# Attention stage of a four-layer graph network: output rows of source nodes made inside the steps, weights taken with the new running maximum

## The chip, the cores and the metric

The kernel runs on one core of a Trainium2 chip. The metric is the device time of one launch in microseconds. Three runs of the kernel before took 2148.57, 2148.97 and 2158.34 us; their median is 2148.97 us.

## The reference, cut to what matters

Four graph layers run one after the other on 10,000 nodes of 512 features and 2,500 edges; each is added to its input and normalised by row. The change is in the last, an attention of 8 heads in which every edge's weight is normalised over the edges that have the same source node:

```python
q, k, v = jnp.split(x @ W, [512, 1024], axis=-1)
aw = jnp.einsum('ehf,ehf->eh', (q * scaling)[src], k[dst])
m = segment_max(aw, src);  e = jnp.exp(aw - m[src])
alpha = e / segment_sum(e, src)[src]
out = segment_sum(alpha[:, :, None] * v[dst], src)
x = layernorm(x + out)          # all 10,000 rows are the output
```

A node that is no edge's source has out = 0, so its row needs none of this.

## The kernel before, in words

**Phases.** Phases follow one another with a barrier between: messages of layer 0, its dense part, `aggregate_phase` and `edge_rows_phase` for layers 1 and 2, and then `values_phase` (names f_), which does the attention. The change is in that last phase, from 1643 us on, but for one loop in `aggregate_phase` that marks which edges are the first of their source (L1103 to L1109, into `k.unique`).

**Two works in one loop.** `values_phase` has `STEPS` = 24 steps. In them run (a) 20 edge tiles of 128 edges, each passing through five stages in five steps (letters a to e in the code, so that tile d of step s is tile s - 3), and (b) 40 pairs of row blocks (2 x 128 rows), the output rows without attention. The edge tiles gather rows of both ends (L1666), finish layer 2 for them (L1976, L1873 to L1881), multiply by W on PE (queries L1770, values L1798, keys L1776), take the scores of 8 heads (L1989), the largest of each source in the tile (L2000, L2006), the weights exp(score - maximum) on ACT (L1906), weighted values (L2017) and their sums per source on PE (L1806).

**A running state in DRAM.** For each source node the table `state` holds 520 sums and 8 maxima. For tile t, POOL gathers the old rows (`gather_state`, L1672), DVE takes the new maximum (L2025), ACT two sets of factors (L1912), DVE scales the old sums and the tile's sums and adds them (L2038 to L2048), and POOL scatters the rows back (`scatter_state`, L1677). The gather of tile t + 1 waits for the scatter of tile t to land. The weights do not wait for the gather.

**Pairs.** `plain_plan` says how many pairs DVE handles in each step: 3, 3, 2, 2, then 2 and 1 in turn, at the end 1 and 2. Four buffers hold them (`ROW_BUFS`). For a pair, SP fills the buffer with a constant row (`pair_fill`, L1224), POOL adds the rows of table p by an accumulating DMA (`pair_add_p`, L1231), DVE scales, rectifies and adds x1 (L1253 to L1272), ACT normalises its two tiles (`tile_normalise`, L1282 to L1287, five operations each), and SP stores it (L1242). A fill waits until the store of the pair four before has landed. The first `PLAIN` = 3 pairs are loaded directly.

**Order.** Every engine works through its own list in order; a wait holds back all that stands behind it. On POOL a step is: scatter of the state, gather of the next state, gathers of rows for two steps on, and the adds for the pairs of the next step, each waiting for its fill. ACT normalises, in a step, tiles of earlier pairs (`tile_plan`): a third early, a third in the middle, and the last one behind the rows of L1881.

**The last loop.** After the steps, ten groups of two tiles follow: POOL gathers the final sums per edge (L1707), DVE divides, adds the residual row and takes its mean and variance (L2083 to L2104), ACT normalises (L1955), and POOL scatters the rows to the output (L1716), where only the first edge of a source writes.

Of the kernel before, what the change touches and what calls it, by code (L numbers as in the profile page):

```python
# [30 lines left out]
P = 128  # L31
# [24 lines left out]
PLAIN = 3  # L56
# [857 lines left out]
def aggregate_phase(nc, k):  # L914
# [4 lines left out]
    with phase(nc, "a_") as (sb, ps, sem), ExitStack() as ctx:  # L919
# [138 lines left out]
        def _(dve):  # L1058
# [44 lines left out]
            ready(nc.vector.memset(seen[:, 0:1], 0.0))  # L1103
# [113 lines left out]
def pair_fill(nc, k, sp, j):  # L1217

    b = j % ROW_BUFS
    if j >= ROW_BUFS:  # L1220
        sp.wait_ge(k.pair_gone[b], 16 * (j // ROW_BUFS))
    else:
        sp.wait_ge(k.quotient_done, 1)
    sp.dma_start(k.pair_rows[b][:, :, :], k.quotient[:, :].rearrange("p (a d) -> p a d", a=1).to_broadcast([P, 2, D])  # L1224
                 ).then_inc(k.pair_filled[b], 16)
# [65 lines left out]
def edge_rows_phase(nc, k):  # L1291

    tail_buffers(nc, k)
    with phase(nc, "e_") as (sb, ps, sem), ExitStack() as ctx:
# [36 lines left out]
        def _(sp):  # L1331
# [11 lines left out]
            pair_fill(nc, k, sp, PLAIN)  # L1343
# [235 lines left out]
def values_phase(nc, k):  # L1579
# [4 lines left out]
    with phase(nc, "f_") as (sb, ps, sem), ExitStack() as ctx:  # L1584
# [19 lines left out]
        fall, factor = sb("fall", [P, 2, HEADS]), sb("factor", [P, 2, HEADS])  # L1604
# [14 lines left out]
        weighed, v_done, vw_done, s_done, old_in, new_top, fall_done, factors, scaled, part_done, merged, gone = (  # L1619
            sem(n) for n in ("weighed", "v_done", "vw", "s_done", "old_in", "new_top", "fall", "factors", "scaled",  # L1620
                             "part", "merged", "gone"))


        G, SUM_BUFS = T // 2, 3
        sums = [k.filters[:, :, :, :].rearrange("p t c f -> p (t c f)")[:, i * 2 * STATE:(i + 1) * 2 * STATE].rearrange(
            "p (s w) -> p s w", s=2) for i in range(SUM_BUFS)]
        inv = [sb(f"inv{i}", [P, 2, HEADS]) for i in range(2)]
        o_stats, o_mv = ([sb(f"o_{n}{i}", [P, 2, w]) for i in range(2)] for n, w in (("stats", 6), ("mv", 2)))
        o_neg, o_rstd, o_shift = ([sb(f"o_{n}{i}", [P, 2]) for i in range(2)] for n in ("neg", "rstd", "shift"))
        sums_in = [sem(f"sums_in{i}") for i in range(SUM_BUFS)]  # L1630
        out_gone = [sem(f"out_gone{i}") for i in range(ROWS_AHEAD)]
        inv_done, att, o_y_done, st, mv_done, o_ready, o_sc, out_done = (
            sem(n) for n in ("inv", "att", "o_y", "st", "mv", "o_ready", "o_sc", "out"))
# [12 lines left out]
        def _(sp):  # L1646
# [10 lines left out]
            for b in range(ROWS_AHEAD):  # L1657
                sp.wait_ge(out_gone[b], 32 * len(range(b, G, ROWS_AHEAD)))

        @block.gpsimd  # L1660
        def _(pool):
# [17 lines left out]

            gather_rows(0)  # L1680
# [8 lines left out]
            for step in range(STEPS):  # L1689
# [7 lines left out]
                if step + 1 < STEPS:  # L1697
                    for j in range(given, given + HERE[step + 1]):
                        pair_add_p(nc, k, pool, j)
                    given += HERE[step + 1]  # L1700
            pool.wait_ge(gone, 16 * T)

            def gather_sums(g):
                if g >= SUM_BUFS:
                    pool.wait_ge(att, 2 * (g - SUM_BUFS + 1))
                for s in range(2):
                    pool.indirect_dma_start(sums[g % SUM_BUFS][:, s, :], None, k.state[:, :],  # L1707
                                            at_rows(k.index[:, 0, 2 * g + s:2 * g + s + 1])
                                            ).then_inc(sums_in[g % SUM_BUFS], 16)

            def scatter_rows(g):
                for s in range(2):
                    t = 2 * g + s
                    pool.wait_ge(out_done, t + 1)

                    pool.indirect_dma_start(k.out[:, :], at_rows(k.unique[:, 1, t:t + 1]), y[g % ROWS_AHEAD][:, s, :],  # L1716
                                            None, bounds_check=N - 1, oob_is_err=False
                                            ).then_inc(out_gone[g % ROWS_AHEAD], 16)

            for g in range(SUM_BUFS):  # L1720
                gather_sums(g)

            for b in range(ROW_BUFS):
                pool.wait_ge(k.pair_gone[b], 16 * (PAIRS // ROW_BUFS))
            for g in range(G):
                if g + SUM_BUFS < G:
                    gather_sums(g + SUM_BUFS)
                scatter_rows(g)

        @block.tensor  # L1730
        def _(pe):
# [50 lines left out]
            def spread_scores(t):  # L1782

                pe.wait_ge(aw_out, t + 1)
                if t:
                    pe.wait_ge(part_done, t)
# [47 lines left out]
        def _(act):  # L1834
# [73 lines left out]
            def state_factors(t):  # L1908
                act.wait_ge(fall_done, t + 1)
                if t:  # L1910
                    act.wait_ge(part_done, t)
                nc.scalar.activation(factor[:, :, :], fall[:, :, :], ACT.Exp).then_inc(factors, 1)  # L1912
# [3 lines left out]
            for step in range(STEPS + 1):  # L1916
# [8 lines left out]
                if 0 <= e < T:  # L1925
                    state_factors(e)
# [23 lines left out]
            for g in range(G):  # L1950
                b, rows = g % 2, y[g % ROWS_AHEAD]
                act.wait_ge(o_ready, g + 1)
                reciprocal_deviation(nc, k, act, o_mv[b][:, :, 1], o_neg[b], o_rstd[b][:, :], o_shift[b], o_sc, 4 * g)
                for s in range(2):
                    nc.scalar.activation(rows[:, s, :], rows[:, s, :], ACT.Identity, bias=o_shift[b][:, s:s + 1],  # L1955
                                         scale=o_rstd[b][:, s:s + 1]).then_inc(out_done, 1)

        @block.vector
        def _(dve):
# [34 lines left out]
            def tile_maximum(t):  # L1994
# [11 lines left out]
                nc.vector.tensor_reduce(top, cand[:, :, :], AX_X, ALU.max).then_inc(top_done, 1)  # L2006
                dve.wait_ge(top_done, t + 1)
                if t:
                    dve.wait_ge(weighed, t)
                nc.vector.tensor_tensor(less[:, :], k.scores[:, t, :], top, ALU.subtract).then_inc(less_done, 1)  # L2010

# [9 lines left out]
            def new_maximum(t):  # L2021
                buf, top = old[t % 2], new[:, ATT:STATE]
                dve.wait_ge(old_in, 16 * (t + 1))
                dve.wait_ge(top_done, t + 1)
                nc.vector.tensor_tensor(top, buf[:, ATT:STATE], buf[:, STATE:STATE + HEADS], ALU.max  # L2025
                                        ).then_inc(new_top, 1)
                dve.wait_ge(new_top, t + 1)
                if t:
                    dve.wait_ge(factors, t)
                nc.vector.tensor_tensor(fall[:, :, :], buf[:, ATT:STATE + HEADS].rearrange("p (a h) -> p a h", a=2),  # L2030
                                        top.rearrange("p (a h) -> p a h", a=1).to_broadcast([P, 2, HEADS]),
                                        ALU.subtract).then_inc(fall_done, 1)

            def merge(t):
                wide = lambda i: factor[:, i, :].rearrange("p (h a) -> p h a", a=1).to_broadcast([P, HEADS, HD + 1])
                dve.wait_ge(factors, t + 1)
                dve.wait_ge(s_done, t + 1)
                nc.vector.tensor_tensor(state_parts(new), state_parts(old[t % 2]), wide(0), ALU.mult  # L2038
                                        ).then_inc(scaled, 1)
                if t:  # L2040
                    dve.wait_ge(merged, t)
                nc.vector.tensor_tensor(
                    part[:, :, :].rearrange("p (a h) f -> p a h f", a=2),
                    p_S[:, :, 0:ATT // 2].rearrange("p a (h f) -> p a h f", h=HEADS // 2),
                    wide(1).rearrange("p (a h) f -> p a h f", a=2), ALU.mult).then_inc(part_done, 1)
                dve.wait_ge(scaled, t + 1)
                dve.wait_ge(part_done, t + 1)
                nc.vector.tensor_tensor(state_parts(new), state_parts(new), part[:, :, :], ALU.add).then_inc(merged, 1)  # L2048

            pair = 0  # L2050
            for step in range(STEPS):
# [3 lines left out]
                if 0 <= e < T:  # L2055
                    new_maximum(e)
# [17 lines left out]

            dve.wait_ge(x3_done, 2 * T)
            for g in range(G):
                b, c, rows = g % 2, g % SUM_BUFS, y[g % ROWS_AHEAD]
# [160 lines left out]
```

## Time and profile before

| what | us |
|---|---|
| median of three runs | 2148.97 |
| the profiled execution | 2156.94 |
| its span, first to last instruction | 2155.2 |
| first pair in `values_phase` | 1643.3 |
| weights of the first edge tile | 1719.0 |
| weights of the last edge tile | 2070.2 |
| start of the last loop's first gather | 2083.8 |

In the profile a row of the timeline is an instruction or several alike in a run; what stands in brackets is how long its engine had been idle and what ended that. In the chain of waits each row was released by the one above it. A DMA's row there lasts from its issue to its landing. PE, ACT, DVE and POOL are compute engines; SP only issues DMAs.

### The profile page before, as it was taken

How to read it: one execution, taken by the hardware profiler on the slowest of the kernel's cores; microseconds unless marked ns; L12 is line 12 of the kernel's file. 1: busy time of each engine (PE TensorE's matmuls, PEld its weight loads, DVE VectorE, ACT ScalarE, POOL GpSimd, SP SyncE). 2: the span in 40 equal slices, each digit the busy share in tenths (PEclk: the TensorE clock that was granted, in tenths of full speed). 3: DMA queues.
4: the chain of work that ended last, by engine and by line, in shares of the span. 5: the costliest groups of instructions: out<-in, count | busy, mean ns of one | idle time of the engine just before them, and what ended most of it. 6: DMA issues, size and time to landing. Idle time of an engine off the chain costs nothing. (4 is left out here: it accounts for less than half of the span.)

```text
span 2155.2 us, 24520 instructions
## 1 busy us (share of the span) xinstructions
PE 1803.9 (84%) x5525; PEld 933.2 (43%) x5525; DVE 1434.7 (67%) x2621; ACT 1149.2 (53%) x2356; POOL 949.1 (44%) x1070
## 2 busy tenths in 40 slices
PE   5999999599999999999999995961881588998840
PEld 2444444244444444444444443531771344544420
DVE  5365554177777777777777773517995578787876
ACT  1344434255555555555555552224883878877853
POOL 2212102166666666656666663544553232333236
PEclk8999999799999999999999997985555689999965
DMA  7752102534444454444444445554556887878774
GB/s 250 250 206 63 27 13 31 142 134 172 171 159 166 157 172 172 165 164 155 169 172 172 163 153 188 105 87 156 110 119 178 257 242 221 238 212 241 200 212 144
DMA packets 167421, 350.61 MB, mean 163 GB/s; under 512 B 30481, under 2 KB 30962, under 8 KB 166838
## 3 DMA queue, kind: packets, MB, share of 16 engines
q1 hardware_dynamic: 130838, 247.28, 32.4%
q0 software_dynamic: 33168, 98.01, 20.4%
q10 hardware_dynamic: 3344, 4.51, 0.7%
q8 instruction: 28, 0.46, 0.1%
q14 instruction: 43, 0.35, 0.1%
HBM read 177.32 MB, written 153.71 MB: 154 GB/s over the span
## 5 line engine op out<-in xcount | busy, mean ns | idle before, releaser
L687 PE MATMUL d_p_h<-w3a,d_xT 128*128 128x512 f32 x632 | 285.6, 595 | 23.2 <-DMA d_xT<-in_xT 23.2
L687 PE MATMUL d_p_p<-d_wr,d_x1T 128*128 128x512 f32 x632 | 288.3, 600 | 0.0
L687 PE MATMUL d_p_o<-d_w,d_uT 128*128 128x512 f32 x632 | 284.5, 593 | 3.0 <-ACT d_uT L762 3.0
L562 POOL TENSOR_SCALAR d_small<-d_mv 128x1 f32<-128x1 f32 x158 | 77.6, 491 | 296.7 <-DVE d_mv L813 148.7
L851 DVE TENSOR_TENSOR d_zz<-d_yg,d_xbeta 128x512 f32<-128x512 f32 x79 | 136.9, 1733 | 96.3 <-POOL d_yg L902 96.3
L687 PEld LDWEIGHTS d_p_h<-w3a,d_xT 128*128 128x128 f32 x632 | 120.7, 191 | 175.6 <-issue 175.6
L687 PEld LDWEIGHTS d_p_o<-d_w,d_uT 128*128 128x128 f32 x632 | 119.8, 190 | 153.7 <-issue 149.1
L755 ACT ACTIVATE d_yn<-d_y,d_small 128x512 f32<-128x512 f32 x79 | 64.3, 814 | 228.2 <-POOL d_small L567 228.2
L687 PEld LDWEIGHTS d_p_p<-d_wr,d_x1T 128*128 128x128 f32 x632 | 115.6, 193 | 116.5 <-issue 116.5
L783 ACT ACTIVATE d_x<-d_zz,d_small 128x512 f32<-128x512 f32 x79 | 64.2, 813 | 174.9 <-POOL d_small L567 174.9
L294 PE MATMUL m_p_H<-m_xT,m_w 128*128 128x512 f32 x320 | 146.8, 613 | 4.8 <-ACT m_xT L335 4.8
L511 DVE TENSOR_SCALAR m_h<-m_p_H,m_bias 128x512 f32<-128x512 f32 x40 | 30.0, 750 | 153.2 <-issue 96.9
L388 ACT ACTIVATE m_den<-m_low 128x512 f32<-128x512 f32 x40 | 25.2, 630 | 188.3 <-DVE m_low L516 188.3
L564 POOL TENSOR_TENSOR d_small<-d_small,minus_half 128x1 f32<-128x1 f32 x158 | 116.1, 735 | 13.2
L1762 PE MATMUL f_p_qv<-filters,same_dst 128*128 128x512 f32 x160 | 88.3, 704 | 32.6 <-ACT same_dst L1842 32.4
L902 POOL TENSOR_TENSOR d_yg<-d_yn,d_gamma_row 128x512 f32<-128x512 f32 x79 | 114.5, 1450 | 0.0
L896 POOL TENSOR_TENSOR d_xb<-d_x,d_b_row 128x512 f32<-128x512 f32 x79 | 100.0, 1266 | 12.5 <-DMA d_x<-in_x 12.5
L221 POOL DMA_INDIRECT sum_counted<-m_tile_sum,unique x20 | 31.4, 1568 | 167.4 <-ACT m_tile_sum L351 150.3
L208 POOL DMA_INDIRECT m_x_in<-in_x,index x40 | 44.3, 1108 | 137.5 <-PE m_p_T L250 123.0
L844 DVE TENSOR_SCALAR d_low<-d_h 128x512 f32<-128x512 f32 x79 | 101.5, 1285 | 2.7
L883 POOL TENSOR_TENSOR d_xbeta<-d_x,d_beta_row 128x512 f32<-128x512 f32 x79 | 100.3, 1270 | 0.0
L806 DVE TENSOR_TENSOR d_y<-d_p_o,d_xb 128x512 f32<-128x512 f32 x79 | 54.6, 691 | 66.9 <-PE d_p_o L687 66.9
(286 smaller groups left out, 4080.9 us busy)
## 6 DMA issues: line engine op xcount, KB each, us to landing
sum_counted<-m_tile_sum SPq DMA_DIRECT2D x10, 2112.0 KB
state<-d_empty SPq DMA_DIRECT2D x80, 264.0 KB, 2.4
update<-d_empty SPq DMA_DIRECT2D x80, 256.0 KB, 2.3
pair_x<-x SPq DMA_DIRECT2D x40, 512.0 KB
out_rows<-pair_rows SPq DMA_DIRECT2D x40, 512.0 KB
d_xT<-in_xT SPq DMA_DIRECT2D x79, 256.0 KB
d_z<-sum_counted SPq DMA_DIRECT2D x79, 256.0 KB
d_x<-in_x SPq DMA_DIRECT2D x79, 256.0 KB
```

What stands on the lines that cost most here:

```text
L294: pe.matmul(out, w1[:, s * KB + b, cols], xT[:, g % 2, s, b, :], start=(s == 0 and b == 0), stop=False)
L562: nc.gpsimd.tensor_scalar(tmp, var, factor, add, ALU.mult, ALU.add).then_inc(done, 1)
L564: nc.gpsimd.tensor_tensor(rstd, tmp, k.minus_half[:, 0:1], ALU.pow).then_inc(done, 1)
L687: last = nc.tensor.matmul(out[:, :], lhsT[:, c, :], w[:, c, :], start=(c == 0), stop=(c == KB - 1))
L755: nc.scalar.activation(yn[b][:, :], y[b][:, :], ACT.Identity, bias=small[b][:, 0, 2:3], scale=small[b][:, 0, 1:2]).then_inc(yn_done, 1)
L783: nc.scalar.activation(x1[b][:, :], zz[b][:, :], ACT.Identity, bias=small[b][:, 1, 2:3], scale=small[b][:, 1, 1:2]).then_inc(x1_done, 1)
L844: nc.vector.tensor_scalar(low[b][:, :], h[b][:, :], MISH_ONE, None, ALU.min).then_inc(low_done, 1)
L851: nc.vector.tensor_tensor(zz[b][:, :], yg[b][:, :], xbeta[b][:, :], ALU.add).then_inc(zz_done, 1)
L883: nc.gpsimd.tensor_tensor(xbeta[b][:, :], x[b][:, :], beta_row[:, :], ALU.add).then_inc(xbeta_done, 1)
L896: nc.gpsimd.tensor_tensor(xb[b][:, :], x[b][:, :], b4_row[:, :], ALU.add).then_inc(xb_done, 1)
L902: nc.gpsimd.tensor_tensor(yg[b][:, :], yn[b][:, :], gamma_row[:, :], ALU.mult).then_inc(yg_done, 1)
L1762: last = nc.tensor.matmul(out[:, :], xT[:, c, :], w[:, c, :], start=(c == 0), stop=(c == KB - 1))
```

## The change

Source rows are finished in the step in which their tile is merged (`attend` on DVE, `source_rows` on ACT), in place in `k.src_rows_sb`; the last loop is gone. `k.unique` now marks the last edge of each source, whose merged sums are final. All output scatters stand in the last three steps of POOL's list (8, 9 and 3 of them), behind a wait for all pair stores, so the pairs are moved to 2 in each of the first 20 steps and none after. The weights of a tile are taken against the new running maximum, so `new_maximum` moves into the step of `tile_maximum`, behind the first pair's means, and the merge is one product and one sum. `PLAIN` is 4.

```diff
 def plain_plan(steps):
-    plan = [3, 3, 2, 2] + [2 - i % 2 for i in range(steps - 6)] + [1, 2]
+    plan = [2] * (steps - 4) + [0] * 4
 def tile_plan(plan):
-        n = given - done if step < 5 or step == len(plan) else min(given - done, 3)
+        n = given - done if step < 5 or step == len(plan) else min(given - done, 4)
 # aggregate_phase, DVE
-            for t in range(1, T):
-                ready(nc.vector.tensor_scalar(equal[:, 0:t * P], rows_i[:, 0:t * P], col_f[:, 0, t:t + 1], None,
+            for t in range(T - 1):
+                later = min((t + 1) * P, LAST_START)
+                ready(nc.vector.tensor_scalar(equal[:, later:E], rows_i[:, later:E], col_f[:, 0, t:t + 1], None,
                                               ALU.is_equal, ALU.add, accum_out=seen[:, t:t + 1]))
 # values_phase, POOL: steps as before, then
+                if step == STEPS - 3:
+                    for b in range(ROW_BUFS):
+                        pool.wait_ge(k.pair_gone[b], 16 * (PAIRS // ROW_BUFS))
+                if step >= STEPS - 3:
+                    for i in range(WRITTEN[step - STEPS + 3], WRITTEN[step - STEPS + 4]):
+                        scatter_out(i)
 # ACT
                 if 0 <= d < T:
                     weights(d)
+                    state_factors(d)
                 if 0 <= b < T:
                     x3_squares(b, 0)
                     x3_squares(b, 1)
                     x3_rows(b)
+                if 0 <= e < T:
+                    source_rows(e)
 # DVE
             def new_maximum(t):
                 dve.wait_ge(old_in, 16 * (t + 1))
...
+                nc.vector.tensor_tensor(less[:, :], k.scores[:, t, :], top, ALU.subtract).then_inc(less_done, 1)
             def merge(t):
+                nc.vector.tensor_tensor(state_parts(new), state_parts(old[t % 2]), wide, ALU.mult).then_inc(scaled, 1)
+                nc.vector.tensor_tensor(halves, halves, p_S[:, :, 0:ATT // 2], ALU.add).then_inc(merged, 1)
+            def attend(t):
+                nc.vector.reciprocal(inv[:, :], state_parts(new)[:, :, HD]).then_inc(inv_done, 1)
...
+                nc.vector.bn_stats(o_stats[b][:, :], row).then_inc(st, 1)
...
                 if 0 <= e < T:
-                    new_maximum(e)
                     merge(e)
...
                 if 0 <= d < T:
+                    new_maximum(d)
                     weigh_values(d)
                 if a < T:
                     softplus(a)
+                if 0 <= e < T:
+                    attend(e)
```

On POOL, one step in the middle before. `f_y` are gathered rows, `pair_rows<-p_rows` the add of a pair, `state<-f_new` the scatter of the state, `f_old<-state` its gather; this step has one add.

```order
L1666 DMA f_y<-update,index 128x512 x2
L1231 DMA pair_rows<-p_rows 128x1024
L1677 DMA state<-f_new,unique 10240x528
L1672 DMA f_old<-state,index 128x528
L1666 DMA f_y<-update,index 128x512 x2
L1231 DMA pair_rows<-p_rows 128x1024 x2
```

The same place in the changed kernel.

```order
L1658 DMA f_y<-update,index 128x512 x2
L1230 DMA pair_rows<-p_rows 128x1024 x2
L1669 DMA state<-f_new,unique 10240x528
L1664 DMA f_old<-state,index 128x528
L1658 DMA f_y<-update,index 128x512 x2
L1230 DMA pair_rows<-p_rows 128x1024 x2
```

Two adds now stand ahead of every scatter of the state up to step 19, where one and two took turns.

On DVE, the middle of a step before, from the tile's candidates to the weighted values (`f_old<-filters` is the tile's maximum, `f_less` what ACT makes weights of).

```order
L2000 TENSOR_TENSOR filters<-f_p_S,f_away 128x1024
L2006 TENSOR_REDUCE f_old<-filters 128x8
L2010 TENSOR_TENSOR f_less<-scores,f_old 128x8
L1269 SCALAR_TENSOR_TENSOR pair_rows,pair_total<-pair_x,pair_rows 128x512 x2
L1272 TENSOR_SCALAR pair_neg<-pair_total 128x2
L2017 TENSOR_TENSOR f_both<-f_p_qv,f_both 128x8x64
```

The same place in the changed kernel, with `attend` behind it.

```order
L1978 TENSOR_TENSOR filters<-f_p_S,f_away 128x1024
L1984 TENSOR_REDUCE f_old<-filters 128x8
L1268 SCALAR_TENSOR_TENSOR pair_rows,pair_total<-pair_x,pair_rows 128x512 x2
L1271 TENSOR_SCALAR pair_neg<-pair_total 128x2
L1991 TENSOR_TENSOR f_new<-f_old 128x8
L1996 TENSOR_TENSOR f_less<-scores,f_new 128x8
L1999 TENSOR_TENSOR f_fall<-f_old,f_new 128x8
L2006 TENSOR_TENSOR f_both<-f_p_qv,f_both 128x8x64
L1942 TENSOR_SCALAR f_pos<-f_y 128x256
L1946 SCALAR_TENSOR_TENSOR f_ssp<-f_logs,f_pos 128x256
L2026 RECIPROCAL f_inv<-f_new 128x8
L2030 TENSOR_TENSOR f_part<-f_new,f_inv 128x8x64
```

`f_less` now reads `f_new`, which reads the gathered `f_old`, and stands behind the pair's means; `attend` begins with the last two rows.

## Rows read from the trace of the kernel before

**Rows 1.** One line's instructions, weights of the 20 edge tiles on ACT (duration, first and last start).

```profile
L1906 ACT ACTIVATE f_both<-f_less x20: 215/216/219, 1719.0 to 2070.2; 128x8 f32<-128x8 f32 x20
```

**Rows 2.** Chain of waits, 1890 to 2040 us (start, time, engine or DMA, what).

```profile
1896.53 6.77 PE f_p_qv L1762 x8
...
2016.13 1.23 DVE filters L2000
...
2026.47 3.71 PE f_p_qv L1762 x8
...
2033.09 1.24 DVE filters L2000
```

**Rows 3.** Chain of waits, 1728 to 1743 us.

```profile
1728.63 5.38 DMA pair_rows<-pair_quotient
1734.30 0.91 POOL pair_rows L1231
1735.51 6.20 DMA state<-f_new,unique
1741.97 1.05 POOL f_old L1672
```

**Rows 4.** Timeline of DVE near 1730 us (start, time, line, what, [idle before]).

```profile
1729.59 0.70 DVE L2048 TENSOR_TENSOR f_new<-f_new,f_part 128x520 f32<-128x520 f32 x1
```

**Rows 5.** Timeline of DVE, first pair of two steps.

```profile
1693.88 1.23 DVE L1253 TENSOR_TENSOR pair_rows<-pair_rows,bn_scale 128x1024 f32<-128x1024 f32 x1 [4.82 <-DMA pair_rows<-p_rows]
...
1711.24 1.23 DVE L1253 TENSOR_TENSOR pair_rows<-pair_rows,bn_scale 128x1024 f32<-128x1024 f32 x1 [4.06 <-DMA pair_rows<-p_rows]
```

**Rows 6.** Timeline of ACT, weights and the step's last row tile.

```profile
2018.85 0.21 ACT L1906 ACTIVATE f_both<-f_less 128x8 f32<-128x8 f32 x1 [0.94 <-DVE f_less L2010]
...
2023.20 0.71 ACT L1282 ACTIVATE pair_scratch<-pair_rows,pair_neg 128x512 f32<-128x512 f32 x1
...
2024.92 0.81 ACT L1287 ACTIVATE pair_rows<-pair_rows,pair_shift,pair_rstd 128x512 f32<-128x512 f32 x1
```

**Rows 7.** Timeline of SP's DMA issues, stores and the fills behind them.

```profile
1794.76 0.34 SPq L1242 DMA_DIRECT2D out_rows<-pair_rows  x1
1797.89 0.60 SPq L1224 DMA_DIRECT2D pair_rows<-pair_quotient  x1
...
1954.57 0.34 SPq L1242 DMA_DIRECT2D out_rows<-pair_rows  x1
1961.64 0.60 SPq L1224 DMA_DIRECT2D pair_rows<-pair_quotient  x1
```

**Rows 8.** Timeline of POOL, an add that waited for a fill.

```profile
1802.25 0.91 POOL L1231 DMA_DIRECT2D pair_rows<-p_rows  x1 [0.62 <-DMA pair_rows<-pair_quotient]
```

**Rows 9.** Line 1707, gathers from the state table in the last loop.

```profile
DMA to landing us min/median/max: 3.3/3.8/4.4
```

**Rows 10.** Line 1666, gathers from the update table during the steps.

```profile
DMA to landing us min/median/max: 3.5/6.1/7.9
```

**Rows 11.** Timeline of DVE, from a tile's weights to the next merge.

```profile
1963.33 0.17 DVE L2010 TENSOR_TENSOR f_less<-scores,f_old 128x8 f32<-128x8 f32 x1
...
1964.87 0.69 DVE L2017 TENSOR_TENSOR f_both<-f_p_qv,f_both 128x512 f32<-128x512 f32 x1
...
1973.49 0.70 DVE L2048 TENSOR_TENSOR f_new<-f_new,f_part 128x520 f32<-128x520 f32 x1
```

**Rows 12.** Timeline of DVE in the last loop, first operation of two groups.

```profile
2089.12 0.28 DVE L2083 RECIPROCAL f_inv<-filters 128x8 f32<-128x8 f32 x2 [2.07 <-DMA filters<-state,index]
...
2093.63 0.27 DVE L2083 RECIPROCAL f_inv<-filters 128x8 f32<-128x8 f32 x2
```

**Rows 13.** Timeline of POOL, the last scatter of output rows.

```profile
2146.48 0.98 POOL L1716 DMA_INDIRECT out_rows<-f_y,unique  x1 [0.31 <-issue]
```

**Rows 14.** Timeline of DVE behind the comparison of source indices.

```profile
1445.33 0.75 DVE L1065 SCALAR_TENSOR_TENSOR column_acc<-dst_rows_sb,share,column_acc 128x512 f32<-128x512 f32 x1 [70.02 <-DMA dst_rows_sb<-p_rows,index]
```

**Rows 15.** Busy times, granted clock and DMA share of a stretch (columns: window, length, PE, PEld, DVE, ACT, POOL, clock, DMA share, GB/s).

```profile
1560.00:1660.00 100.00, 58.05 (x266) 51.80 (x266) 70.21 (x147) 59.91 (x144) 48.30 (x39) 0.56 0.59 141
```

More of the change, by code:

```diff
@@ L55 @@
 ROW_BUFS = 4
-PLAIN = 3
+PLAIN = 4
 STATE = ATT + HEADS
@@ L1219, in pair_fill @@
     b = j % ROW_BUFS
[L1220 to L1223, printed above, removed]
+    sp.wait_ge(k.pair_gone[b], 16 * (j // ROW_BUFS))
     sp.dma_start(k.pair_rows[b][:, :, :], k.quotient[:, :].rearrange("p (a d) -> p a d", a=1).to_broadcast([P, 2, D])
@@ L1342, in _ @@
                 pair_load_x1(nc, k, sp, j)
-            pair_fill(nc, k, sp, PLAIN)
             sp.wait_ge(scattered, 16 * T)
@@ L1603, in values_phase @@
         new, part = sb("new", [P, STATE]), sb("part", [P, HEADS, HD + 1])
-        fall, factor = sb("fall", [P, 2, HEADS]), sb("factor", [P, 2, HEADS])
+        fall, factor = sb("fall", [P, HEADS]), sb("factor", [P, HEADS])
         p_T = [ps(f"p_T{i}", [P, D]) for i in range(2)]
@@ L1618, in values_phase @@
         top_done, less_done, heads_set = (sem(n) for n in ("top", "less", "heads_set"))
-        weighed, v_done, vw_done, s_done, old_in, new_top, fall_done, factors, scaled, part_done, merged, gone = (
+        weighed, v_done, vw_done, s_done, old_in, new_top, fall_done, factors, scaled, merged, gone = (
             sem(n) for n in ("weighed", "v_done", "vw", "s_done", "old_in", "new_top", "fall", "factors", "scaled",
[L1621 to L1633, printed above, removed]
+                             "merged", "gone"))
+        inv = sb("inv", [P, HEADS])
+        o_stats, o_mv = ([sb(f"o_{n}{i}", [P, w]) for i in range(2)] for n, w in (("stats", 6), ("mv", 2)))
+        o_neg, o_rstd, o_shift = ([sb(f"o_{n}{i}", [P, 1]) for i in range(2)] for n in ("neg", "rstd", "shift"))
+        inv_done, att, o_y_done, st, mv_done, o_ready, o_sc, out_done, out_gone = (
+            sem(n) for n in ("inv", "att", "o_y", "st", "mv", "o_ready", "o_sc", "out", "out_gone"))
+        WRITTEN = (0, 8, T - 3, T)
         HERE = plain_plan(STEPS)
@@ L1656, in _ @@
             pair_store(nc, k, sp, PAIRS - 1)
-            for b in range(ROWS_AHEAD):
-                sp.wait_ge(out_gone[b], 32 * len(range(b, G, ROWS_AHEAD)))
+            sp.wait_ge(out_gone, 16 * T)
         @block.gpsimd
@@ L1678, in scatter_state, with scatter_out @@
                                         ).then_inc(gone, 16)
+            def scatter_out(t):
+                pool.wait_ge(out_done, t + 1)
+                pool.indirect_dma_start(k.out[:, :], at_rows(k.unique[:, 1, t:t + 1]), k.src_rows_sb[:, t, :], None,
+                                        bounds_check=N - 1, oob_is_err=False).then_inc(out_gone, 16)
             gather_rows(0)
@@ L1697, in _ @@
                 if step + 1 < STEPS:
-                    for j in range(given, given + HERE[step + 1]):
+                    for j in range(max(given, PLAIN), given + HERE[step + 1]):
                         pair_add_p(nc, k, pool, j)
                     given += HERE[step + 1]
[L1701 to L1728, printed above, removed]
+                if step == STEPS - 3:
[4 more added lines that the diff above has]
+                        scatter_out(i)
         @block.tensor
@@ L1785, in spread_scores @@
                 if t:
-                    pe.wait_ge(part_done, t)
+                    pe.wait_ge(merged, t)
                 else:
@@ L1910, in state_factors, with source_rows @@
                 if t:
-                    act.wait_ge(part_done, t)
-                nc.scalar.activation(factor[:, :, :], fall[:, :, :], ACT.Exp).then_inc(factors, 1)
+                    act.wait_ge(scaled, t)
+                nc.scalar.activation(factor[:, :], fall[:, :], ACT.Exp).then_inc(factors, 1)
+            def source_rows(t):
+                b, row = t % 2, k.src_rows_sb[:, t, :]
+                act.wait_ge(o_ready, t + 1)
+                reciprocal_deviation(nc, k, act, o_mv[b][:, 1:2], o_neg[b], o_rstd[b][:, :], o_shift[b], o_sc, 3 * t)
+                nc.scalar.activation(row, row, ACT.Identity, bias=o_shift[b][:, 0:1], scale=o_rstd[b][:, 0:1]
+                                     ).then_inc(out_done, 1)
             nc.scalar.preload_act_table_set(ACT_SET)
@@ L1924, in _ @@
                     x3_turned_out(c, 1)
-                if 0 <= e < T:
-                    state_factors(e)
                 if 0 <= b < T:
@@ L1949, in _ @@
                 unit += TILES[step]
[L1950 to L1956, printed above, removed]
         @block.vector
@@ L2006, in tile_maximum, with new_maximum @@
                 nc.vector.tensor_reduce(top, cand[:, :, :], AX_X, ALU.max).then_inc(top_done, 1)
+            def new_maximum(t):
+                buf, top = old[t % 2], new[:, ATT:STATE]
+                dve.wait_ge(old_in, 16 * (t + 1))
                 dve.wait_ge(top_done, t + 1)
+                nc.vector.tensor_tensor(top, buf[:, ATT:STATE], buf[:, STATE:STATE + HEADS], ALU.max
+                                        ).then_inc(new_top, 1)
+                dve.wait_ge(new_top, t + 1)
                 if t:
@@ L2010, in tile_maximum @@
                 nc.vector.tensor_tensor(less[:, :], k.scores[:, t, :], top, ALU.subtract).then_inc(less_done, 1)
+                if t:
+                    dve.wait_ge(factors, t)
+                nc.vector.tensor_tensor(fall[:, :], buf[:, ATT:STATE], top, ALU.subtract).then_inc(fall_done, 1)
             def weigh_values(t):
@@ L2019, in weigh_values @@
                                         ).then_inc(vw_done, 1)
[L2021 to L2027, printed above, removed]
-                if t:
[L2029 to L2039, printed above, removed]
-                if t:
[L2041 to L2048, printed above, removed]
+            def merge(t):
+                wide = factor[:, :].rearrange("p (h a) -> p h a", a=1).to_broadcast([P, HEADS, HD + 1])
+                dve.wait_ge(factors, t + 1)
+                nc.vector.tensor_tensor(state_parts(new), state_parts(old[t % 2]), wide, ALU.mult
+                                        ).then_inc(scaled, 1)
+                dve.wait_ge(scaled, t + 1)
+                dve.wait_ge(s_done, t + 1)
+                halves = new[:, 0:ATT].rearrange("p (a w) -> p a w", a=2)
+                nc.vector.tensor_tensor(halves, halves, p_S[:, :, 0:ATT // 2], ALU.add).then_inc(merged, 1)
@@ new lines, in attend @@
+            def attend(t):
+                b, row, mean = t % 2, k.src_rows_sb[:, t, :], part[:, :, 0:HD]
+                dve.wait_ge(merged, t + 1)
+                if t:
+                    dve.wait_ge(att, t)
+                nc.vector.reciprocal(inv[:, :], state_parts(new)[:, :, HD]).then_inc(inv_done, 1)
+                dve.wait_ge(inv_done, t + 1)
+                if t:
+                    dve.wait_ge(o_y_done, t)
+                nc.vector.tensor_tensor(mean, state_parts(new)[:, :, 0:HD],
+                                        inv[:, :].rearrange("p (h a) -> p h a", a=1).to_broadcast([P, HEADS, HD]),
+                                        ALU.mult).then_inc(att, 1)
+                dve.wait_ge(att, t + 1)
+                nc.vector.tensor_tensor(row.rearrange("p (h f) -> p h f", h=HEADS), mean,
+                                        row.rearrange("p (h f) -> p h f", h=HEADS), ALU.add).then_inc(o_y_done, 1)
+                dve.wait_ge(o_y_done, t + 1)
+                if t >= 2:
+                    dve.wait_ge(out_done, t - 1)
+                nc.vector.bn_stats(o_stats[b][:, :], row).then_inc(st, 1)
+                dve.wait_ge(st, t + 1)
+                nc.vector.bn_aggr(o_mv[b][:, :], o_stats[b][:, :]).then_inc(mv_done, 1)
+                dve.wait_ge(mv_done, t + 1)
+                nc.vector.tensor_scalar(o_neg[b][:, :], o_mv[b][:, 0:1], -1.0, None, ALU.mult).then_inc(o_ready, 1)
@@ L2073, in _ @@
                 pair += HERE[step]
-            dve.wait_ge(x3_done, 2 * T)
-            for g in range(G):
-                b, c, rows = g % 2, g % SUM_BUFS, y[g % ROWS_AHEAD]
-                heads = [sums[c][:, s, 0:ATT].rearrange("p (h f) -> p h f", h=HEADS) for s in range(2)]
-                dve.wait_ge(sums_in[c], 32 * (g // SUM_BUFS + 1))
-                if g >= 2:
-                    dve.wait_ge(att, 2 * g - 2)
-                for s in range(2):
-                    nc.vector.reciprocal(inv[b][:, s, :], heads[s][:, :, HD]).then_inc(inv_done, 1)
-                dve.wait_ge(inv_done, 2 * g + 2)
-                if g >= ROWS_AHEAD:
-                    dve.wait_ge(out_gone[g % ROWS_AHEAD], 32 * (g // ROWS_AHEAD))
-                for s in range(2):
-                    nc.vector.tensor_tensor(
-                        rows[:, s, :].rearrange("p (h f) -> p h f", h=HEADS), heads[s][:, :, 0:HD],
-                        inv[b][:, s, :].rearrange("p (h a) -> p h a", a=1).to_broadcast([P, HEADS, HD]), ALU.mult
-                        ).then_inc(att, 1)
-                dve.wait_ge(att, 2 * g + 2)
-                nc.vector.tensor_tensor(rows[:, :, :], rows[:, :, :], k.src_rows_sb[:, 2 * g:2 * g + 2, :], ALU.add
-                                        ).then_inc(o_y_done, 1)
-                dve.wait_ge(o_y_done, g + 1)
-                if g >= 2:
-                    dve.wait_ge(out_done, 2 * g - 2)
-                for s in range(2):
-                    nc.vector.bn_stats(o_stats[b][:, s, :], rows[:, s, :]).then_inc(st, 1)
-                for s in range(2):
-                    dve.wait_ge(st, 2 * g + s + 1)
-                    nc.vector.bn_aggr(o_mv[b][:, s, :], o_stats[b][:, s, :]).then_inc(mv_done, 1)
-                dve.wait_ge(mv_done, 2 * g + 2)
-                nc.vector.tensor_scalar(o_neg[b][:, :], o_mv[b][:, :, 0], -1.0, None, ALU.mult).then_inc(o_ready, 1)
 def attended_rows_phase(nc, k):
```

2 lines of the change are left out of this document (1 added, 1 removed).

## The prediction

> **What bounds the kernel now.** I read the page's slices first: the reader is to see that PE is nearly full up to the attention phase and that from 1643 us on no engine is. Then the weights of the 20 edge tiles, one small ACT operation per step and so a clock of the steps: the first starts at 1719.0 us and the last at 2070.2 us, 18.5 us a step [rows 1]. I write W for that moment in a step. Behind the last W come 85.0 us to the end of the span, most of them the last loop.
>
> The chain of waits says what a step hangs on. With nothing late it is a ring through DVE, ACT and PE: from one tile's candidates to the next tile's, 2016.13 to 2033.09 us, 17.0 us [rows 2]. ACT's share of it holds three tiles of pairs. The rest of the 18.5 us is waits for pairs. In one place the chain leaves the engines: a fill, POOL's add, the scatter of the state, its gather [rows 3]. DVE had ended that merge at 1730.29 us [rows 4], yet the scatter was issued at 1735.51 us, right behind the add. POOL had stood 5 us at the add's wait for a fill, and the scatter, next in its list, stood with it. Before, a step of slack covers this, since the gathered rows are first read at the merge, one step after the weights. This is the place that decides the change.
>
> **The change part by part.**
>
> *Last loop out, output scatters into the last steps.* Of the 85.0 us behind the last W stay: weighted values, sums and merge, some 4 us (an estimate, four operations of about 0.7 us with hand-overs), one attend, half of a group of two that took 4.51 us, so 2.3 us [rows 12], ACT's four operations, 1.7 us (a pair's tile of 2.53 us less its squaring pass of 0.71 us and that pass's read-out [rows 6]), three scatters at 1.3 us, and the 8.7 us that lay between the last scatter's issue and the end [rows 13]. That is 20 us: 65 us less.
>
> *First steps.* Before, eight pairs and the ninth's first half lie ahead of the first W; now six and the seventh's. The seventh began at 1693.88 us and the ninth at 1711.24 us, W 7.8 us later [rows 5]. The means of that pair now stand ahead of W, 1.5 us [rows 11]. So W of the first tile is at 1693.9 + 7.8 + 1.5 = 1703 us, 16 us earlier.
>
> *Weights behind the gather.* Now W of a tile needs the new maximum, this the gathered rows, these the scatter of the tile before. Follow it from W of step s. On ACT, W to the start of the step's last tile took 4.35 us and that tile to its end 2.53 us [rows 6]; state factors (0.1 us) and the source rows (1.7 us) now stand between: 8.7 us. That tile belongs to the second pair of step s - 1. Its store is issued, and the buffer's fill only when the store has landed: 3.1 us in one case, 7.1 us in another [rows 7]. The fill that began at 1797.89 us let POOL's add go at 1802.25 us: 4.4 us [rows 7, 8]; in the chain it took 5.7 us to the add [rows 3]. This add is for step s + 1, and POOL's list has the scatter of the state right behind it: 1.2 us on, at 1735.51 after 1734.30 [rows 3]. The merge it waits for is long done (below), so it goes at once. Scatter to gather took 6.5 us behind an add [rows 3]. The gather's landing is not shown in the steps, where nobody waited for it. The nearest rows are 3.3 to 4.4 us for the same table in the last loop [rows 9] and 3.5 to 7.9 us, median 6.1 us, for rows of another table beside the pairs [rows 10]. I take 4.5 us, since in a longer step the queues are emptier than those of rows 10 but not as empty as in the last loop; the ends are 3.3 and 6.1 us. New maximum, difference and hand-over to ACT are 0.5 us, and that is W of step s + 1. The ring is 8.7 + 3.1 + 4.4 + 1.2 + 6.5 + 4.5 + 0.5 = 28.9 us. With the shorter gather it is 27.7 us, with the longer store, fill and gather 35.8 us.
>
> For two rows of this sum the Trainium skill has a smaller figure: its page "DMA: Bandwidth & Descriptors", section "Anatomy of one DMA", fits a DMA issued from GpSimd with 2.0 us and its bytes at 436 GB/s. For 270 KB that would be an estimate of 2.6 us for the scatter and as much for the gather, and the ring 23.1 us. The trace does not agree: the scatter's row is 6.5 us.
>
> The ring holds where adds stand ahead of the scatter, from the first tile's W (step 3) to that of step 19: 16 times, 462 us. Then there are three steps without adds. The first still has the second pair's DVE work and four tiles on ACT, and I give it 22 us (the DVE ring below); the others 19.5 us and 19 us, the 17.0 us of today plus source rows and, on POOL, eight scatters of 1.3 us.
>
> *What else grows, and is covered.* The engines' own ring gets one more tile (2.5 us), the source rows (1.7 us), the pair's means (1.5 us) and 0.3 us of small operations on top of 17.0 us: 23.0 us. The DVE ring: from weighting to the end of the next merge it took 9.3 us [rows 11]; less one product of 0.7 us and small ones, plus 2.3 us of attend, some 10.5 us, then scatter, gather and maximum, 12 us: 22.5 us. Both lie under 28.9 us and cost nothing as long as that stands; without it they set 23.0 us. DVE's loop over the source indices keeps its 19 operations at 4% fewer columns, and DVE idles 70.02 us behind it [rows 14]: nothing. The one pair that is loaded instead of filled and added saves one add, which is in the first steps' count.
>
> *Sum.* 1703 + 462 + 60.5 + 20 = 2245.5 us of span; the profiled execution lies 1.7 us over its span, so 2247 us, against 2156.94 us. That execution lies 8.0 us above the median of the runs, so I forecast 2239 us: 90 us slower. From the first W to the last it is 522.5 us against 351 us, 171 us more; the loop and the first steps give back 81 us.
>
> **Rivals.**
>
> *A: the buffer comes back in time and the scatter is not held.* Then the engines' ring of 23.0 us sets the step: 1703 + 368 + 60.5 + 20 + 1.7 - 8.0 = 2145 us, not slower. It decides if store, fill, scatter and gather together take under 12.6 us instead of 18.5 us. For it speaks that a longer step loads the queues less. Against it, the least that rows 3, 7, 8 and 9 show together is 17.3 us. By the Trainium skill's figure above for scatter and gather the sum would be 12.7 us, at this point.
>
> *B: PE at its lower clock decides.* Eight matmuls took 6.77 us in one step and 3.71 us in another [rows 2]. From 1560 to 1660 us, with PE busy 58 of 100 us, the granted clock was 0.56, mostly the 1.2 GHz level [rows 15]. A step of 28.9 us with PE's present work is about as empty. The queries lie in the engines' ring, so it would be 23.0 + 3.1 = 26.1 us, under 28.9 us; it decides only if the DMA part is some 3 us shorter than I say, and gives 2239 - 16 x 2.8 = 2194 us. The Trainium skill's page "TensorE: Matmul & The Clock Gate", section "Why this matters for your kernels", says the same: gaps between bursts of matmuls bring the lower level back.
>
> *C: the DMAs of this ring land as late as the latest rows.* Then it is 35.8 us and the time 2239 + 16 x 6.9 = 2349 us. Two pairs a step are more transfers in the same order; against it, the step is longer too, so that there are fewer per microsecond than now.
>
> **How the numbers follow.** My forecast (a ring of 27.7 to 32 us, 2220 to 2289 us) has 0.64, A 0.11, B 0.11, C and what lies between 0.14. The range of 2185 to 2310 us leaves out A and the upper half of C. Less than 0.5% (11 us) can't be told from no change. A lies 0.2% under the median; of its 0.11 I give 0.06 to the same and 0.05 to faster. All else is slower: 0.89.
>
> **What would show it.** In the changed profile W should come every 28 to 30 us from its second to its seventeenth time, and faster after. DVE should wait at the new maximum for the gather of the state, ACT at the weights for DVE. POOL's scatter of the state should start right behind an add that had waited for a fill, with the merge done several us before. The chain of waits should go ACT tile, store, fill, add, scatter, gather, maximum. If the scatter is released by the merge instead, A or B holds and I am wrong in the mechanism; if PE ends most waits of the new maximum's step, it is B. About 20 us should lie between the last W and the end.

## The result and the profile after

The changed kernel takes 2222.59 us (median of 4 runs, 2222.02 to 2224.66 us), against 2153.65 us of the kernel before (median of 4 runs, 2148.57 to 2158.47 us): a ratio of 1.0315, 95% interval 1.0295 to 1.0335. That is 69 us slower. Forecast were 2239 us and 2185 to 2310 us.

The first row below is the weights' line as in [rows 1], with what ACT waited for there. The next is DVE's new maximum, with what DVE waited for: the gather of the state, in 17 of 20 steps. The last is POOL's line of adds on the page (busy, mean ns, idle time ahead of it and its releaser).

```profile
L1883 ACT ACTIVATE f_both<-f_less x20: 215/216/217, 1705.9 to 2200.2; 128x8 f32<-128x8 f32 x20
its engine sat idle before it (us, times) until:
  DVE f_less L1996: 141.0, 20
...
L1991 DVE TENSOR_TENSOR f_new<-f_old x20: 166/167/169, 1705.5 to 2199.8; 128x8 f32<-128x8 f32 x20
...
  DMA f_old<-state,index: 84.8, 17
...
L1230 POOL DMA_DIRECT2D pair_rows<-p_rows x36 | 34.5, 959 | 277.1 <-DMA pair_rows<-pair_quotient 277.1
```

From the first W to the last it is now 494.3 us, against 351.2 us [rows 1]: 143.1 us more. The first W is 13.1 us earlier, and the way from the last W to the end falls from 85.0 to 20.5 us. Together the span grows by 65.5 us, to 2220.7 us. Single intervals from W to W are 26.5 to 28.6 us in the sixteen steps, 27.43 us in the mean (their ends are 1705.91 and 2144.72 us); then come 20.85, 20.61 and 14.04 us.

One whole step in the chain of waits, from a W at 2061.82 us to the next (start, time, engine or DMA, what):

```profile
2061.82 0.02 ACT f_both L1883
...
2067.15 0.81 ACT src_rows_sb L1895
2067.97 0.71 ACT pair_scratch L1281 x2
...
2069.59 0.82 ACT pair_rows L1286
...
2070.43 2.63 DMA out_rows<-pair_rows
2073.06 0.02 issue
2073.08 3.37 DMA pair_rows<-pair_quotient
2076.45 0.30 issue
2076.75 0.90 POOL pair_rows L1230
2077.64 0.30 issue
2077.95 6.27 DMA state<-f_new,unique
2084.21 0.26 issue
2084.47 4.23 DMA f_old<-state,index
2088.70 0.02 issue
2088.73 0.18 DVE f_new L1991
...
2089.13 0.02 ACT f_both L1883
```

The chain is tile, store, fill, add, scatter, gather, maximum, in the order of the prediction. No row of it is PE's. POOL's timeline of the same step shows how the scatter came into it (start, time, what, idle time ahead of it):

```profile
2076.75 0.90 POOL L1230 DMA_DIRECT2D pair_rows<-p_rows  x1 [14.51 <-DMA pair_rows<-pair_quotient]
2077.95 1.05 POOL L1669 DMA_INDIRECT state<-f_new,unique  x1 [0.30 <-issue]
2084.47 1.05 POOL L1664 DMA_INDIRECT f_old<-state,index  x1 [5.48 <-DMA state<-f_new,unique]
```

And on DVE's timeline the merge that this scatter carries:

```profile
2072.11 0.69 DVE L2018 TENSOR_TENSOR f_new<-f_new,f_p_S 128x520 f32<-128x520 f32 x1
```

The merge ended at 2072.80 us, the scatter left at 2077.95 us. POOL had stood 14.51 us at the add's wait for a fill, and the scatter behind it waited 5.1 us with its data ready: the picture of [rows 3, 4], now without the step of slack. In all sixteen steps the scatter leaves 0.30 or 0.31 us behind such an add, 5.1 to 7.6 us after its merge has ended.

### The profile page after: what moved, and what is told of

It reads as the page before. It is cut to its first block and busy times, and to the rows that moved or that the text cites. A ratio compares the mean times of both kernels' runs of the same rounds, so it can differ in the third digit from the quotient of the medians.

```text
span 2220.7 us, 24512 instructions
## 1 busy us (share of the span) xinstructions
PE 1849.9 (83%) x5525; PEld 955.9 (43%) x5525; DVE 1427.9 (64%) x2622; ACT 1152.8 (52%) x2376; POOL 911.8 (41%) x1049
## 5 line engine op out<-in xcount | busy, mean ns | idle before, releaser
L1739 PE MATMUL f_p_qv<-filters,same_dst 128*128 128x512 f32 x160 | 115.5, 887 | 57.6 <-ACT same_dst L1819 57.6
L1230 POOL DMA_DIRECT2D pair_rows<-p_rows x36 | 34.5, 959 | 277.1 <-DMA pair_rows<-pair_quotient 277.1
```

What stands on the lines that cost most here:

```text
L1739: last = nc.tensor.matmul(out[:, :], xT[:, c, :], w[:, c, :], start=(c == 0), stop=(c == KB - 1))
```

## The experiments

Each ratio below is to the kernel before as timed beside that run (medians of 2156.78 us for the first three runs and 2157.42 us for the others), so times of different runs, taken against each other, are good to a few us only.

**The scatter out of the add's shadow.** The second add of each step goes behind the gather.

```diff
                     if t + 1 < T:
                         gather_state(t + 1)
+                if held is not None:
+                    pair_add_p(nc, k, pool, held)
+                    held = None
...
                     for j in range(max(given, PLAIN), given + HERE[step + 1]):
-                        pair_add_p(nc, k, pool, j)
+                        if j == given + 1:
+                            held = j
+                        else:
+                            pair_add_p(nc, k, pool, j)
```

> The second add of each step is issued by POOL one step later, right behind the gather of the state, instead of ahead of the scatter of the state; all else as in the changed kernel. My theory (the scatter stands in POOL's list behind an add that waits for a fill): the interval from W to W falls from 27.4 us to the engines' own ring of about 23 us, the scatter is released by the merge, and the scatter takes nearer 3.0 us than 6.5 us; 16 x 4.4 = 70 us less, 2150 to 2165 us. Rival (the ring is set by DVE, the gather and the scatter themselves, whatever stands ahead of the scatter): the interval stays within 1 us of 27.4 us, 2205 to 2225 us. Second rival (the add, now later, makes DVE wait for the second pair): the interval is 25 to 27 us, DVE's longest waits are at the second pair, 2185 to 2215 us.

Measured: 2165.49 us, just over the range of my theory, ratio to the kernel before 1.0037 (1.0020 to 1.0055). W to W is 23.67 us over the sixteen steps. POOL's scatter is now released by the merge:

```profile
1930.54 1.74 POOL L1669 DMA_INDIRECT state<-f_new,unique  x1 [10.99 <-DVE f_new L2024]
1936.83 1.08 POOL L1664 DMA_INDIRECT f_old<-state,index  x1 [4.54 <-DMA state<-f_new,unique]
```

The hold was worth some 57 us. But scatter to gather is 6.29 us here, with no add just ahead of it, so the expected 3.0 us did not come. The chain has gone over to the engines:

```profile
1924.56 0.81 ACT src_rows_sb L1901
1925.37 0.71 ACT pair_scratch L1281 x2
...
1928.54 6.73 PE f_p_qv L1745 x8
...
1936.09 2.05 PE f_p_S L1773 x16
1938.13 5.32 PE f_p_qv L1745 x8
...
1944.98 0.70 DVE f_part L2036
1945.70 0.70 DVE src_rows_sb L2040
1946.43 0.70 DVE f_o_stats L2045
```

The queries take 6.73 us, the slow duration of [rows 2]. Behind the values (the 5.32 us) stand the attend on DVE and the source rows on ACT, and only then the last tile and the next step.

**The tile's own maximum again.** One part undone: the difference is taken to the tile's maximum, and the merge needs two products as before. The source rows stay in the steps, and so do two pairs in each.

```diff
                 nc.vector.tensor_reduce(top, cand[:, :, :], AX_X, ALU.max).then_inc(top_done, 1)
+                dve.wait_ge(top_done, t + 1)
+                nc.vector.tensor_tensor(less[:, :], k.scores[:, t, :], top, ALU.subtract).then_inc(less_done, 1)
...
                 if 0 <= e < T:
+                    new_maximum(e)
                     merge(e)
...
                 if 0 <= d < T:
-                    new_maximum(d)
                     weigh_values(d)
```

> The weights are taken with the tile's own maximum as before (difference behind the tile's maximum, two factors, two products in the merge, new maximum one step later), while the source rows in each step, the scatters of the output and two pairs in each step stay. My theory (the loss is the ring of weights, store, fill, add, scatter and gather, which this edit opens by a step of slack): W to W is 20 to 22.5 us, set by the engines or by the pairs' DMAs, 16 x 5 to 7.4 us less, 2100 to 2140 us, faster than both kernels. Rival (the loss is the two pairs and the source rows that each step now holds, whatever the maximum): W to W stays 26 us or more, 2200 to 2225 us.

Measured: 2160.22 us, ratio 1.0015 (0.9991 to 1.0040), W to W 22.83 us. The step became shorter, as my theory had it, but it stopped just over the top of my range; the time came out 20 us above it, and not below the kernel before. The chain says why. The weights no longer wait for the gather, but POOL's list is as it was: all sixteen scatters still leave 0.30 or 0.31 us behind an add that had waited for a fill. What pays for it now are the pairs. The gather waits for the late scatter, the next step's first add stands behind the gather, and DVE waits for its pair:

```profile
1917.59 6.25 DMA out_rows<-pair_rows
1923.86 3.74 DMA pair_rows<-pair_quotient
...
1927.90 0.90 POOL pair_rows L1230
...
1929.10 6.06 DMA state<-f_new,unique
...
1935.42 1.05 POOL f_old L1664
...
1938.98 7.30 DMA pair_rows<-p_rows
1946.28 0.02 issue
1946.30 1.24 DVE pair_rows L1252
```

From 1800 to 2000 us the chain goes this way four times, from stores at 1803.14, 1848.08, 1917.59 and 1962.45 us, and through the engines in between.

**Two pairs alone.** The kernel before with the new plan of pairs and nothing else.

```diff
-    plan = [3, 3, 2, 2] + [2 - i % 2 for i in range(steps - 6)] + [1, 2]
+    plan = [2] * (steps - 4) + [0] * 4
...
-        n = given - done if step < 5 or step == len(plan) else min(given - done, 3)
+        n = given - done if step < 5 or step == len(plan) else min(given - done, 4)
```

> The kernel before with one part of the change alone: two pairs in each step and none in the last four (up to four tiles of pairs in a step), the weights and the last loop as before. My theory: W to W goes from 18.5 us to 20 to 21.5 us over sixteen steps and the last steps get shorter, and the loop behind them stays, so 2140 to 2190 us. Rival (two pairs in a step are themselves what fills a step to 27 us): 2230 to 2290 us.

Measured: 2187.22 us, ratio 1.0126 (1.0098 to 1.0154), W to W 21.89 us, a little over the range I gave for it, and the time inside. So the parts can be put in a row by their ratios: two pairs in each step +1.3%; source rows into the steps and the last loop out, on top of that, -1.1%; weights with the new maximum, on top of both, +3.0%.

**Five buffers.** The add keeps its place ahead of the scatter; its buffer comes free earlier. Five buffers with nothing shared were tried first and gave no time: they leave 480 B per partition of the on-chip memory (SBUF) where another tensor needs 2048 B. So ACT's scratch row is shared here.

```diff
-ROW_BUFS = 4
+ROW_BUFS = 5
...
-                if ROW_BUFS <= j + 3 < PAIRS:
-                    pair_fill(nc, k, sp, j + 3)
+                if ROW_BUFS <= j + 4 < PAIRS:
+                    pair_fill(nc, k, sp, j + 4)
```

> The changed kernel with five buffers for pairs instead of four (ACT's scratch row is shared to make the room), and each fill behind the store of the pair five ahead of it instead of four; POOL's list as in the changed kernel, with the adds ahead of the scatter of the state. The second add of a step then waits for a store that ended some 15 us before W. My theory (the hold of the scatter is the wait for the buffer, not the order of POOL's list by itself): W to W falls to the ring that the run with the adds behind the gather showed, 23 to 24.5 us, and the time to 2155 to 2175 us. Rival (the add itself, or its transfer, holds the scatter even where its buffer is free): W to W stays over 26 us, 2200 to 2225 us.

Measured: 2163.74 us, ratio 1.0028 (1.0010 to 1.0046), W to W 23.17 us, and 23.9 us in the later steps, as in the first experiment. POOL's list is that of the changed kernel, yet the add waits 1.09 us, and the scatter is released by the merge:

```profile
1909.23 0.90 POOL L1233 DMA_DIRECT2D pair_rows<-p_rows  x1 [1.09 <-DMA pair_rows<-pair_quotient]
1921.09 1.77 POOL L1673 DMA_INDIRECT state<-f_new,unique  x1 [10.96 <-DVE f_new L2022]
```

So it was the wait for the buffer that held the scatter; the order of the list only passed it on. Either edit takes it away.

**Attend and source rows early.** On top of the first experiment, DVE's attend goes ahead of the residual and ACT's source rows ahead of the logarithms.

```diff
+                if 0 <= e < T:
+                    attend(e)
                 if 0 <= b < T:
                     residual(b)
...
-                if 0 <= e < T:
-                    attend(e)
...
+                if 0 <= e < T:
+                    source_rows(e)
                 if a < T:
                     logarithms(a)
...
-                if 0 <= e < T:
-                    source_rows(e)
```

> The kernel with the adds behind the gather, and in addition DVE's attend put behind the merge and the first leaky operation of the step, and ACT's source rows ahead of the logarithms, so that neither stands between the values and the next step. My theory (with the hold gone a step of 23.9 us is the chain through PE at its lower clock, weighting, attend, source rows, last tile): it loses 2.9 us of attend and 1.7 us of source rows until ACT's own work, some 20 us a step, stops it: W to W 20.5 to 22 us, 2110 to 2140 us. Rival (the chain closes at once another way, by the state's scatter and gather or by the pairs' store, fill and add): W to W 22.5 us or more, 2145 to 2170 us.

Measured: 2117.44 us, ratio 0.9829 (0.9793 to 0.9866), W to W 21.12 us. The 23.9 us were the chain through values, attend, source rows and last tile. Not all of the gain is the moved work itself: in the shorter step the granted clock from 1740 to 2040 us is 0.90 instead of 0.78, and the queries take 5.40 us or less in most steps instead of 6.7 us.

**Both on five buffers.** The same early places on the five buffers, once with the tile's own maximum and once with the new maximum of the change.

> The tile's own maximum as before, with five buffers for pairs and the attend and source rows put early; two pairs in each step and the source rows in each step stay. My theory (with four buffers this kernel was set by the ring of tile, store, fill, add, 22.8 us a step): the ring opens and ACT's own work sets 20 to 21 us, 2100 to 2125 us, faster than the kernel before by over 1%. Rival (the pairs' DMAs themselves, not the buffers, set the step): 22 us or more, 2140 to 2160 us.

Measured: 2118.23 us, ratio 0.9830 (0.9794 to 0.9865), W to W 20.94 us.

> The changed kernel (weights with the new maximum) with five buffers for pairs and the attend and source rows put early; POOL's list as in the changed kernel. My theory: both waits that were found are gone, W to W is 20.5 to 22 us, 2110 to 2140 us, and faster than the kernel before; what the new maximum itself costs is then the difference to the run with the tile's own maximum, 0 to 1 us a step. Rival (the ring of sums, merge, scatter, gather and maximum is itself longer than the engines' work): 22.5 us or more, 2145 to 2170 us.

Measured: 2115.65 us, ratio 0.9825 (0.9786 to 0.9864), W to W 20.86 us. It is the changed kernel in all its parts, faster than both kernels, and can't be told from the run with the tile's own maximum: with the wait gone, the new maximum costs nothing that these runs show. Busy times from 1740 to 2040 us, of the changed kernel and of this one (columns as in [rows 15]):

```profile
1740.00:2040.00 300.00, 212.63 (x645) 114.78 (x645) 200.40 (x404) 202.30 (x545) 66.38 (x66) 0.78 0.68 193
```

```profile
1740.00:2040.00 300.00, 253.39 (x850) 135.21 (x849) 263.45 (x534) 265.39 (x716) 93.31 (x83) 0.90 0.85 247
```

DVE and ACT go from two thirds busy to 88%. The wait for the gather is small now: at the new maximum DVE waits 8.0 us for it, against 84.8 us, and ACT at the weights waits 30.8 us in all, against 141.0 us. The ring is covered, not gone: scatter and gather of the state still make 29% of the chain from 1740 to 2040 us.

```profile
L1887 ACT ACTIVATE f_both<-f_less x20: 215/216/219, 1704.7 to 2089.9; 128x8 f32<-128x8 f32 x20
its engine sat idle before it (us, times) until:
  DVE f_less L2000: 30.8, 20
```

## Why the prediction was right

**The sign and the mechanism.** The ring of the prediction is the chain of the trace, link by link. Sixteen scatters leave 0.30 or 0.31 us behind an add that had waited for a fill, and the two edits that free them, one in POOL's order and one in the number of buffers, each give back 57 to 59 us.

**The sum.** The span was forecast at 2245.5 us and is 2220.7 us, 24.8 us less. The sixteen steps make 23.2 us of that (438.8 against 462 us), the last three 5.0 us (55.5 against 60.5 us); the first W came 2.9 us later than forecast, and the way to the end is 0.5 us longer. In the step shown, the terms are:

- tile on ACT 8.6 us (forecast 8.7)
- store 2.65 us (3.1)
- fill to add 3.67 us (4.4)
- add to scatter 1.20 us (1.2)
- scatter to gather 6.52 us (6.5)
- gather 4.26 us (4.5)
- maximum to W 0.40 us (0.5)

They add up to 27.3 us, against 28.9 us. The mis-sized terms are store, fill and gather, 1.4 us together: I had taken them from rows of a denser stretch [rows 7, 8, 10] (from 1740 to 2040 us the DMA engines are busy 0.79 of the time before and 0.68 now), and weighed the emptier queues of a longer step for the gather alone; that this is the reason was not tested. My forecast also came down by 8 us, by which the profiled execution of before lay above the median of three runs. That step was wrong, and helped by luck: the kernel before has medians of 2156.78 and 2157.42 us in 19 and 13 later runs, so its profiled execution of 2156.94 us was an ordinary one. Without the 8 us I would have said 2247 us.

**Where the gains went.** The loop and the earlier first W gave back 64.5 + 13.1 = 77.6 us (81 us forecast), and the steps took 143.1 us.

**Three readings of the trace of before** were off, and none of them decided the result. POOL had stood 7.50 us, not 5 us, at the add of [rows 3]; some 5 us is what the scatter waited with its data ready. The chain leaves the engines in more than one place: pair adds, such as one of 9.00 us at 1947.95 us, make 15.2% of it from 1720 to 2070 us, and the state's scatters 10.2%. And PE was nearly full in the steps, busy 270.71 of 300 us:

```profile
1734.30 0.91 POOL L1231 DMA_DIRECT2D pair_rows<-p_rows  x1 [7.50 <-DMA pair_rows<-pair_quotient]
...
1740.00:2040.00 300.00, 270.71 (x958) 148.49 (x957) 237.03 (x462) 240.59 (x647) 96.61 (x86) 0.94 0.79 226
```

**Rival A** needed store, fill, scatter and gather in under 12.6 us together; they took 17.1 us. Two runs made it true by hand, and it then gives 2164 to 2165 us, not 2145 us: its step is 23.2 to 23.7 us instead of 23.0 us, its first W at 1705.6 and 1707.0 us instead of 1703 us, and the 8 us that I took off for the median were not there. That the step came so near 23.0 us is luck in part: I had priced that ring with queries of 3.71 us, and the one of the first experiment holds slow queries and goes another way (rival B).

**Rival B** is half right. PE's slow queries decide nothing in the changed kernel: the granted clock is 0.78 in the steps, a mean between its levels of 1.2 and 2.4 GHz, and no PE row stands in the chain from the first W to the seventeenth. Once the hold is gone they do stand in the chain, 6.73 us of 23.9 us in the first experiment. The 26.1 us that I gave for it counted too much: with these queries, and at the same mean clock of 0.78, the step was 23.9 us. In that run the chain goes from the queries over the values to attend, past the candidates, the pair's means and W, which I had all put into one ring.

**Rival C** did not come: the longest step is 28.6 us. The long store that it was built on (7.1 us) is nearly there in the run with the tile's own maximum (6.25 us), where the steps are shorter.

**What I did not see.** I priced the engines' ring, 23.0 us, as the floor under the hold, and did not ask whether attend and source rows had to stand in it. They had not: the same work at an earlier place in each step is worth 48 us more, with four buffers and with five, the faster PE that came with it included.

## What to carry to other kernels

A wait on an in-order queue is paid by everything behind it. When a change takes away a step of slack, look in the chain for the places where an instruction with its data ready starts right behind another one's wait, and price the whole ring that closes there. Before giving up such a change, free the wait (one more buffer, or the waiting instruction behind the urgent one) and move work that nobody waits for out of the ring that is left.

## What the runs showed of the hardware

I had put the 6.5 us of the scatter to its place behind an add. The runs don't bear that out: it depends on what else is under way. In the changed kernel's last steps, where neither adds nor fills run, scatter to gather takes 3.00 to 3.03 us, as here:

```profile
2155.98 0.98 POOL L1669 DMA_INDIRECT state<-f_new,unique  x1 [14.14 <-DVE f_new L2018]
2159.00 0.97 POOL L1664 DMA_INDIRECT f_old<-state,index  x1 [2.04 <-DMA state<-f_new,unique]
```

In the first experiment SP issues a fill and a load of 512 KB each beside the scatter at 1930.54 us, and scatter to gather takes 6.29 us:

```profile
1930.49 0.61 SPq L1223 DMA_DIRECT2D pair_rows<-pair_quotient  x1
1931.14 0.61 SPq L1236 DMA_DIRECT2D pair_x<-x  x1
```

With attend early the fill comes 0.2 to 1.2 us after the scatter in five of the sixteen steps, and scatter to gather takes 5.6 to 6.7 us there. In nine steps the fill comes 2.6 to 3.3 us after it, and although an add was issued some 4 us ahead, scatter to gather takes 3.5 to 4.2 us, here 3.68 us:

```profile
1860.87 1.02 POOL L1669 DMA_INDIRECT state<-f_new,unique  x1 [3.13 <-DVE f_new L2024]
1864.55 1.21 POOL L1664 DMA_INDIRECT f_old<-state,index  x1 [2.66 <-DMA state<-f_new,unique]
```

So the figure of some 2.6 us that the Trainium skill's page "DMA: Bandwidth & Descriptors", section "Anatomy of one DMA", gives by its fit (an estimate) is near an undisturbed scatter here (3.0 us to the next issue), and less than half of one beside two transfers of 512 KB. Whether the bytes or the order in the queues make the difference was not tried.
